# First image group loaded before the tables and folded by VectorE; six fillers in place of three ahead of the slot inversion

## The reference

```python
f = fftshift(fft2(images)); f = f[192 x 192 around the centre]; power = abs(f)
tokens = (power sorted by radius, 16 bins of 2304 points x 3 channels) @ W + b     # 64 x 16 x 192
h = concat([cls, tokens]) + sinusoidal_pe                                          # 64 x 17 x 192
h = layernorm(h + causal_attention(h))            # 12 heads of 16
x = h + attention(layernorm(h))                   # 12 heads, not causal
t = layernorm(x)
logits = t @ gate_w.T + gate_b                    # 8 experts, the best 2 of each token
for e in range(8):
    out += cw[:, e:e+1] * (gelu(t @ w1[e].T + b1[e]) @ w2[e].T + b2[e])
return layernorm(h + (x + out))
```

## Time and profile before

| | |
|---|---|
| median of 3 runs | 886.38 us |
| lowest and highest run | 877.69 and 886.82 us |
| the profiled execution | 886.28 us |
| its span, first to last instruction | 884.4 us |
| spectrum, PE's first to last pass | 10.31 to about 304 us |
| gathers of the rings | 336.6 to 566 us |
| router, from the first expert logits to the first row transposes | 714.7 to 747.9 us |
| PE busy | 759.8 us, 86% of the span |
| PE's mean granted clock | 0.924 of full speed |

### The profile page before, as it was taken

The page is one execution under the profiler, slowest core; times in us unless marked ns, Lnnn a source line. Parts: engine busy times, 40 slices in busy tenths (PEclk is TensorE's granted clock), DMA queues, the critical chain, the costliest instruction groups (busy, mean ns, idle before and its releaser), DMA issues. The chain is left out here.

```text
span 884.4 us, 16768 instructions
## 1 busy us (share of the span) xinstructions
PE 759.8 (86%) x5845; PEld 648.5 (73%) x5846; DVE 527.6 (60%) x988; ACT 432.7 (49%) x840; POOL 454.8 (51%) x371
## 2 busy tenths in 40 slices
PE   5999999999999702598787977999899998999996
PEld 5888888888888501498786866967557775899995
DVE  4899999999999603254434542769848764222213
ACT  1777777777777801234333532524133321555561
POOL 4578777778777506676576656300242033444420
PEclk9999999999999955789898978999999987999997
DMA  9744548855688276444444445220000473111103
GB/s 235 220 123 131 140 117 245 221 151 143 175 239 250 121 209 174 132 139 129 120 140 116 116 117 142 73 74 2 2 1 2 188 213 108 50 53 52 46 26 115
DMA packets 72986, 111.71 MB, mean 126 GB/s; under 512 B 8391, under 2 KB 52396, under 8 KB 72556
## 3 DMA queue, kind: packets, MB, share of 16 engines
q1 hardware_dynamic: 60014, 75.66, 30.1%
q0 software_dynamic: 11776, 34.62, 13.8%
q10 hardware_dynamic: 1152, 0.84, 0.3%
HBM read 91.04 MB, written 20.06 MB: 126 GB/s over the span
## 5 line engine op out<-in xcount | busy, mean ns | idle before, releaser
L551 PE MATMUL psum<-power,tT 128*128 128x192 f32 x864 | 169.9, 355 | 81.4 <-DVE tT L663 61.7
L551 PEld LDWEIGHTS psum<-power,tT 128*128 128x128 f32 x864 | 157.5, 209 | 91.4 <-issue 70.6
L492 POOL DMA_INDIRECT rows<-power_table,rank_row x144 | 147.6, 1025 | 102.0 <-issue 41.6
L295 PE MATMUL ps<-dft,fold 112*112 112x97 f32 x1536 | 170.2, 265 | 18.5 <-POOL fold L262 10.3
L295 PEld LDWEIGHTS ps<-dft,fold 112*112 112x112 f32 x1536 | 164.5, 180 | 27.2 <-DVE folded L367 15.3
L269 POOL TENSOR_TENSOR ss<-uv 97x388 f32<-97x388 f32 x96 | 119.4, 1266 | 77.9 <-ACT uv L335 77.9
L663 DVE SCALAR_TENSOR_TENSOR tT<-rows,swaps,scaled 128x384 f32<-128x384 f32 x144 | 81.3, 613 | 93.0 <-remote 45.8
L367 DVE TENSOR_TENSOR folded<-ps,far 112x388 f32<-112x388 f32 x192 | 98.6, 554 | 18.2 <-ACT far L323 18.2
L262 POOL TENSOR_TENSOR fold<-img 112x896 f32<-112x896 f32 x48 | 101.9, 2123 | 12.4 <-DMA img<-in_x 6.8
L602 ACT ACTIVATE scaled<-rows,swaps 128x384 f32<-128x384 f32 x144 | 77.7, 604 | 60.5 <-DMA rows<-power_table,rank_row 44.9
L384 DVE TENSOR_TENSOR uv<-ps,odd 97x388 f32<-97x388 f32 x192 | 98.6, 555 | 14.3 <-ACT odd L328 12.7
(11 more groups left out here) (177 smaller groups left out, 956.1 us busy)
## 6 DMA issues: line engine op xcount, KB each, us to landing
img<-in_x SPq DMA_DIRECT2D x48, 784.0 KB, 5.1
power_table<-power SPq DMA_DIRECT2D x16, 576.0 KB
power<-in_w_tok SPq DMA_DIRECT2D x3, 1728.0 KB, 10.4
power_table<-power SPq DMA_DIRECT2D x1, 4656.0 KB
power<-in_w SPq DMA_DIRECT2D x8, 579.0 KB, 7.8
power<-in_w SPq DMA_DIRECT2D x4, 1152.0 KB, 10.7
rows<-power_table,rank_row POOLq DMA_INDIRECT x144
expert_inputs<-normed SPq DMA_DIRECT2D x3, 288.0 KB, 2.3
```

Of the source, the lines that this page charges most:

```text
L295: last = pe.matmul(ps1[0:HALF, j % 2, i, col:col + FREQ], fold[:, j // UPG % FOLD_RING, part, x0:x0 + HALF], dft[:, part * FREQ:(part + 1) ...
L492: pool.indirect_dma_start(out=rows[:, j % RING, half, :], out_offset=None, in_=table[0:RECORDS if j < PLAIN else ROWS, :], in_offset=bass. ...
L551: last = pe.matmul(ps[:, q % 2, 0:DIM], points[:, j % SWAPPED, c, s].rearrange("p h b -> p (h b)"), wt[:, c, s, chunk, :], start=(chunk == ...
```

## The change

Four things are changed. On SP, the first image group is issued first of all, `dft` second, then the other three groups, and `rank_row` and `swaps` only after them. On DVE, the sum of group 0 is computed right behind its difference (new line 401), and it counts `fold_done`. On POOL, step 0 no longer folds; it waits until `fold_done` is 1, so that its own counts keep their meaning. On PE, six fillers in place of three stand ahead of the slot inversion.

```diff
     def program_sync(sp):
-        sp.dma_start(dft[:, :], dft_in).then_inc(dft_in_s, 16)
         sp.sem_inc(root_room, R_GROUPS)
...
         for g in range(Y_RING):
             load(g, g)
+            if g == 0:
+                sp.dma_start(dft[:, :], dft_in).then_inc(dft_in_s, 16)
         load_constants(sp)
...
         def step(t, j):
-            if not isinstance(t, int) or t < GROUPS:
+            if isinstance(t, int) and t == 0:
+                pool.wait_ge(fold_done, 1)
+            elif not isinstance(t, int) or t < GROUPS:
                 fold_group(t, j)
...
         fold_odd(0, 0)
+        dve.tensor_tensor(fold[:, 0, 0], img[:, 0, 0], img[:, 0, 1], ALU.add).then_inc(fold_done, 1)
         pipeline(dve, step, BODY_U, [(BODY_U, UNITS - BODY_U, BODY_U)], UNITS + ODD)
...
         last.then_inc(cw_tr, 1)
-        busy_work(pe, W, psum[:, 6, :], 3)
+        busy_work(pe, W, psum[:, 6, :], 6)
         pe.wait_ge(numbers_set, 1)
...
         def load_constants(sp):
+            sp.dma_start(rank_row[:, :], a["rank_row"]).then_inc(index_in, 16)
+            sp.dma_start(swaps[:, :, :], a["swaps"]).then_inc(index_in, 16)
             for dst, src in loads:
                 sp.dma_start(dst, src).then_inc(loaded, 16)
...
         @block.sync
         def _(sp):
-            sp.dma_start(rank_row[:, :], a["rank_row"]).then_inc(index_in, 16)
-            sp.dma_start(swaps[:, :, :], a["swaps"]).then_inc(index_in, 16)
             spec[0](sp)
```

## The result

| | before | changed kernel |
|---|---|---|
| median | 885.57 us (20 runs) | 879.71 us (20 runs) |
| lowest and highest run | 877.69 and 888.97 us | 875.78 and 884.72 us |
| profiled execution | 886.28 us | 879.88 us |
| its span | 884.4 us | 878.1 us |

The ratio of the times is 0.9944, with a 95% interval of 0.9927 to 0.9962. That is 5.0 us (3.4 to 6.5) off 885.57; the two medians lie 5.9 us apart, inside that interval. The forecast was 881.0 in a range of 873 to 887, and the sum of the two gains was 5.3 us.

The account below looks back on a forecast made before the run. Bound by a chain of load, folds and PE at the start, and in the router by DVE, POOL, PE waits with the clock falling in the inversion. 886.28 - 2.1 (start) - 3.2 (fillers) = 881.0 us, range 873 to 887.

Parts of the forecast that it names:

- (a): Start, SP's queue: first image group issued at 0.73 instead of 2.20, so it lands 1.47 us earlier, at about 5.7.
- (b): Start, folds of group 0: DVE does both in 2.2 us, so PE starts at about 8.0, 2.3 us earlier.
- The prediction's upper end: Start, first landing: 2.0 us earlier if the 0.3 MB that went ahead had also held its data back.
- (c): PE's first 48 passes: a 2.3 us half-rate cost stays, up to 1.5 us more or less; no change taken.
- (d): Spectrum, fifth group: its load lands at 26.7 to 27.2 and caps the start's lead; 2.1 us taken.
- The fillers: Router, ahead of the inversion: three more fillers keep the clock full, inversion 4.2 us for 7.46; gain 3.2 us.
- Rival 2: Router: clock falls in the middle or at the head of the inversion; 881.9 or 884.3 us; chance 0.15.
- the prediction's line on those fillers: Router, behind the inversion: four fillers, as slow again, end at 744.8, against 744.6 for the rows.
- Rival 3: Start: fifth group lands at 28.2 and caps the lead at 1.0 us, time 882.1 us; chance 0.08.
- Rivals 4 and 5: Rings: more waits make it slower, 887.2 or 890.3 us, chance 0.08; or the other way, 872.4 us, chance 0.22.
- the stretch of gathers: Rings, first gather to last: forecast counted wrong if more than 5 us off its 230.

Follow-up runs that it names:

- the start alone: The changed kernel with three fillers ahead of the inversion in place of six: 885.1 us, ratio 0.9963 to the kernel before.
- the repeat on the second chip: The changed kernel itself, nothing altered, measured again on another chip: 885.83 us, ratio 0.9972 to the kernel before.
- The early issue: The changed kernel with the fifth image group issued after 12 of the 31 small transfers: 880.96 us, ratio 0.9915 to the kernel before.

## Why the prediction held, step by step

The total came 1.3 us under the forecast. Of that, 0.7 is its base, 886.28 where 20 runs have a median of 885.57, and 0.6 is the gain, 5.9 us between the medians for 5.3. The two mechanisms were as said; within them some steps were wrong, and that the start came out so near was in part luck.

- **(a) and (b), the start.** Said: group 0 lands at 5.7 and PE starts at 8.0. Measured: 5.75 and 7.95. The two parts were also right apart: the folds give 0.93, said 0.9, and the order 7.19 - 5.75 = 1.44, said 1.47. Between kernels on the other chips it was 1.8 (7.81 to 6.04) and 2.1 (8.48 to 6.42), though the issue moved by the same 1.39 (2.20 to 0.81) on all. The prediction's upper end, that what went ahead also held the data back, is neither shown nor ruled out by this: on one chip the same start varied by up to 0.6. The start of DVE's first fold lay between 5.75 and 6.81 in nine profiles of the new order, and between 7.19 and 8.48 in three of the old. That `dft` costs nothing behind the image group held too.
- **(c), the first 48 passes.** Said: no change in the first 48. They took 7.44 and then 7.00, and 6.80 to 8.14 in the other kernels. It is a scatter of over 1 us in which the change cannot be seen, and it belongs in the range.
- **(d), the fifth group.** The stall is there and the kept lead is 2.5 to 2.65 in place of 2.1, but the working had two errors that worked against each other, and that is luck. SP came to the group later than said, at 22.82 for 22.11, so DVE waited 1.60 us, not 0.3. The moment scatters whatever the order: 22.09 to 24.64 in the profiles with the image group first and the late issue, and 22.11 to 23.92 in three with the old order. The prediction took it as fixed. Against this, the lead was not lost one for one at DVE. What PE waits for is POOL's fold, called covered in the prediction; the earlier trace rows already show it ending at 31.54 + 2.09 = 33.63, only 0.14 ahead of PE's start. PE starts 3.2 us behind the landing. Worked out from that, a landing at 27.2 would have allowed 33.77 - 30.4 = 3.4 us of lead, no cap at all, and only the later issue made one.
- **The fillers.** Said: six without a gap, a wait of 0.6, an inversion of 4.2 us, transposes 9.5 behind `numbered`. Measured: a wait of 0.66, then 4.43 and 9.82. The 3.2 us are 2.95. Over all kernels the inversion took 7.46, 7.86, 7.66 and 7.01 us with three fillers, 4.43, 4.51, 4.88, 4.51, 4.97 and 4.57 with six, and 4.20 with nine. The transposes came 12.77, 14.37, 13.02 and 12.71 behind `numbered` with three, and with six 9.82, 9.83, 11.10, 9.85, 11.10 and 9.91.
- **Rival 2, the clock falls within the inversion.** It came in part: the fall is at about 736.0, one or two passes before the end. It costs at most 4.43 - 4.20 = 0.2 us there, not 0.9. In the two inversions of 4.88 and 4.97 us it fell five or six passes before the end, and the four slow fillers behind then kept PE from rows that had landed. Together that took 1.3 us of the gain (11.10 for 9.8), more than the rival's price; the prediction's line on those fillers (744.8 against 744.6) had seen how close they were. The 207 ns of the prediction is an average with some five quick passes in it; a slow pass takes 213. PE had no gap from 731.92 on, and its clock fell to 1.2 GHz. The Trainium skill ("TensorE: Matmul & The Clock Gate", Why this matters for your kernels) says that unbroken work keeps the full clock; this trace does not agree.
- **Rival 3**, a harder cap, is what the start alone and the repeat on the second chip showed: leads at the gathers of 2.27 and 2.08. There it was no 1.0, but with nine fillers, on the same start, the lead was lost altogether. The rival priced the wait alone, not the clock behind it. The early issue removes both.
- **Rivals 4 and 5, the rings.** Between the two profiles they differ by 0.65 us. Across kernels they scatter: 239.4 to 245.7 us, once 236.6, on the first three chips. Said: the stretch of gathers stays within 5 us of 230. It went from 228.7 to 226.1.

## What to carry to other kernels

A lead won at the head of a pipeline is worth what the next late arrival leaves of it: find the first transfer that is issued behind a fixed queue, and follow its landing through every engine that folds it, to the one that ends last. A stall there can cost more than its length, if the clock falls in it (3.2 us behind one of 2.15 here). A filler ahead of a wait costs nothing while it ends before what is waited for, and can be worth more than the wait (3 us for three fillers here); one too many delays the work directly, and those behind it can hold up the next arrival (1.3 us in two of six profiles). Where a later stage scatters by more than the gain, read the gain from the moments in the trace, and use medians of many runs only to confirm it.

## What the runs showed of the hardware

**TensorE's clock fell during the inversion, with PE at work.** From the start of one pass to the start of the next, a pass of 24 columns took 112 ns at 2.4 GHz and 213 at 1.2 (the inversions of 4.20 and 7.46 us). Behind an idle stretch of 3.2 us the clock fell after 2 to 10 of the 36 passes (four profiles with three fillers) and did not come back in the inversion. Behind six fillers it stood for 30 to 35 of them and then fell (0.99 over 734 to 736 in the changed kernel, 0.50 behind it), with PE busy throughout. Behind nine it stood through all 36 and fell in the fillers that followed. With a filler between the pieces it stood.

**The same fall comes in the last stage, on three of four chips.** There the 9 matmuls of 8 rows (18 passes), two fillers and the last sum took 3.19 + 1.98 + 6.21 = 11.4 us in the four profiles of the second chip, and 3.57 + 3.78 + 7.40 = 14.8 in that of before, 3.89 + 3.78 + 7.08 = 14.8 in that of after. On the third chip they took 13.0 to 14.8, on the fourth 13.0 and 13.6. So the two profiles are alike in it, but it is worth up to 3.4 us. Whether it goes by the chip or by the execution is open, with one profile of each kernel. Windows of the changed kernel there:

```profile
858.00:860.00 2.00, 2.00 (x11) 1.88 (x9) 0.00 (x0) 0.01 (x1) 0.00 (x0) 0.71 0.98 310
860.00:862.00 2.00, 2.00 (x4) 0.84 (x3) 0.00 (x0) 0.00 (x0) 0.00 (x0) 0.50 1.11 335
```

**The rings are 38 us shorter on one chip.** First gather to last turn is 241.0 us in the changed kernel on the first chip and 203.0 on the fourth. A gather takes the same on both, 1016 and 1013 ns. 33.5 of the 38.0 us are POOL's waiting for DVE, 34.4 us there and here:

```profile
POOL rows L496 <- DVE tT L667: 0.9, 3, 0.3
```

On the other chips this wait and the length of the rings go together as well: 30.3 us of it in the shortest (236.6), 39.3 in the longest (245.7). The windows of 380 to 420 us, first chip and then fourth:

```profile
380.00:420.00 40.00, 33.97 (x182) 33.26 (x181) 17.96 (x31) 14.80 (x28) 26.13 (x27) 0.86 0.45 128
```

```profile
380.00:420.00 40.00, 34.91 (x213) 32.29 (x211) 22.17 (x34) 19.32 (x38) 30.55 (x32) 1.00 0.54 153
```

The clock stands at 1.00 on the fourth chip from 380 to 530 us and swings between 0.67 and 0.99 on the first. So the two go together. Whether the fall of the clock starts the waits, or the waits the fall, no run here tells apart, and why one chip escapes it stays open. It would be worth more than all that was tried here.

**The clock record begins late.** The first unit's 16 passes took 3.3 us, half rate, where 16 take 1.72 later, though the windows give 1.00 at 10 to 18 us.
